# First pair's rows, key projections, query products and statistics computed in the setup's last stretch, whose steps get another order

## The reference

```python
def xattn(q, k, v, ...):                      # q = layernorm(x), k = v = ctx; layer_norm inside has gain and bias
    proj = lambda t: split_heads(layer_norm(t, ln_g, ln_b) @ w_in.T)       # 8 heads of 128
    f_q, f_k, f_v = proj(q), proj(k), proj(v)
    cosine_sim = einsum(f_q, f_k) / (|f_q| |f_k|)
    q_ratio, k_ratio = 2 * min(var, 1) / (var + 1) of f_q and f_k, per row and head
    var_component = q_ratio (x) k_ratio
    feat_corr = off-diagonal of (centered f_q)^T (centered f_q) / rows     # over ALL rows, per head
    decorr_scale = exp(-5 * norm(feat_corr) / D^2)
    h1 = relu(layer_norm([mean f_q, mean f_k] @ wp_w1.T + wp_b1)); weights = softmax(h1 @ wp_w2.T + wp_b2)
    mixed = w0 * cosine_sim + w1 * cosine_sim * decorr_scale + w2 * var_component
    return (mixed @ f_v) @ w_out.T + b_out
x = x + tanh(g_xattn) * xattn(layernorm(x), ctx, ctx)
x = x + tanh(g_ffn) * ffn(layernorm(x))       # 16-head softmax attention over pairs of batches (512 rows), two l2
                                              # normalisations and a gelu behind it
```

## Time and profile before

| | us |
|---|---|
| median of 3 runs (1323.11 to 1327.89) | 1324.99 |
| the profiled execution, its own time | 1325.61 |
| its span | 1323.9 |
| PE busy in the span | 1186.1 (90%) |
| DVE busy | 1066.7 (81%) |
| ACT busy | 1008.6 (76%) |
| POOL busy | 291.5 (22%) |

### The profile page before, as it was taken

The page is one execution under the profiler, slowest core; times in us unless marked ns, Lnnn a source line. Parts: engine busy times, 40 slices in busy tenths (PEclk is TensorE's granted clock), DMA queues, the critical chain, the costliest instruction groups (busy, mean ns, idle before and its releaser), DMA issues.

```text
span 1323.9 us, 34712 instructions
## 1 busy us (share of the span) xinstructions
PE 1186.1 (90%) x10322; PEld 748.6 (57%) x10322; DVE 1066.7 (81%) x3084; ACT 1008.6 (76%) x3333; POOL 291.5 (22%) x257
## 2 busy tenths in 40 slices
PE   4999967899999989898989898989898989898865
PEld 2677546564656565656565555656565656564521
DVE  5986635788888897988888888988888889898864
ACT  5768213296969696969797978888887889797887
POOL 1444103212212130303131212122222222222200
PEclk9999877999999999999999999999999999999987
DMA  8450014272727181818181827263635454454550
GB/s 259 135 168 22 4 37 96 89 168 83 186 67 202 48 221 42 213 46 216 45 212 37 207 59 203 66 190 79 181 88 170 99 159 110 148 121 147 108 160 17
DMA packets 247888, 162.30 MB, mean 123 GB/s; under 512 B 94538, under 2 KB 235559, under 8 KB 247848
## 3 DMA queue, kind: packets, MB, share of 16 engines
q1 hardware_dynamic: 247848, 161.80, 45.6%
HBM read 86.74 MB, written 42.58 MB: 98 GB/s over the span
## 4 chain that ended last, share of the span: by engine, by line
PE 66%; ACT 10%; issue 6%; DVE 3%; DMA 1%; ACTq 0%; SPq 0%; POOL 0%; POOLq 0%; PEldq 0%; DVEq 0%
PE work L894 18%; PE work L896 16%; PE work L895 16%; PE attended L1448 8%; PE score L1437 4%; ACT prob L1534 3%; PE work L1345 2%; ACT L1534 1%; ACT L1558 1%; ACT Gh L1507 1%; ACT zb L1558 1%; DVE wqTl L1634 1%; ACT wqTh L1493 1%; ACT VTh L1507 1%; ACT v L1520 1%
## 5 line engine op out<-in xcount | busy, mean ns | idle before, releaser
L1534 ACT ACTIVATE prob<-score,nm 128x256 f32<-128x256 f32 x1024 | 481.4, 495 | 18.6 <-DVE nm L1731 14.7
L1731 DVE TENSOR_REDUCE nm<-score 128x2 f32<-128x512 f32 x512 | 336.8, 680 | 9.3 <-PE score L1437 9.0
L1534 ACT ACTIVATION_READ_ACCUMULATOR prob<-score,nm 128x1 f32 x1024 | 232.7, 227 | 0.0
L1591 POOL TENSOR_TENSOR mTl<-md,mTh 128x512 f16<-128x512 f32 (+1 forms) x96 | 95.2, 998 | 357.9 <-ACT mTh L1507 357.9
L1448 PE MATMUL attended<-prob,vsp 128*32 128x256 f32 x2048 | 137.4, 392 | 1.9 <-DVE vsp L1746 1.0
L1649 DVE BATCH_NORM_STATS2 qst<-work 128x6 f32<-128x128 f32 x512 | 111.5, 281 | 12.0 <-PE work L896 11.9
L1437 PE MATMUL score<-qstack,kstack 64*128 64x256 f16 x1024 | 97.5, 279 | 18.7 <-ACT prob L1534 13.0
L1603 POOL TENSOR_TENSOR nrs<-nrm,phalf 128x8 f32<-128x8 f32 x16 | 26.3, 1642 | 352.7 <-ACT zb L1554 352.7
L894 PE MATMUL work<-wTh,xTh 128*128 128x512 f16 x256 | 98.1, 383 | 6.1 <-DVE xTl L1643 3.5
L895 PE MATMUL work<-wTl,xTh 128*128 128x512 f16 x256 | 97.8, 382 | 0.0
L896 PE MATMUL work<-wTh,xTl 128*128 128x512 f16 x256 | 97.8, 382 | 0.0
(11 more groups left out here) (327 smaller groups left out, 3216.4 us busy)
## 6 DMA issues: line engine op xcount, KB each, us to landing
qstack<-parts SPq DMA_DIRECT2D x64, 256.0 KB, 3.3
kstack<-parts SPq DMA_DIRECT2D x64, 256.0 KB, 3.8
sqE<-sq_rows SPq DMA_DIRECT2D x64, 154.0 KB
s_xin<-in_x SPq DMA_DIRECT2D x8, 1024.0 KB, 6.1
xin<-in_x SPq DMA_DIRECT2D x16, 512.0 KB, 3.6
x2S<-in_x SPq DMA_DIRECT2D x16, 512.0 KB, 3.6
parts<-qh SPq DMA_DIRECT2D x32, 256.0 KB, 2.5
parts<-ql SPq DMA_DIRECT2D x32, 256.0 KB, 2.7
```

Source lines behind the costliest of these rows:

```text
L1534: nc.scalar.activation(prob[:, g % PG, e, j + jj, :], sc[n % SC][:, jj * NQ:(jj + 1) * NQ], ACT.Exp, bias=nm[:, u + jj:u + jj + 1], accum_ ...
L1591: nc.gpsimd.tensor_tensor(dst, src, emptied(e[:2], "h")[0], ALU.subtract).then_inc(m_ready, 1)
L1731: nc.vector.tensor_reduce(nm[:, u:u + 2], sc[n % SC][:, :].rearrange("p (u q) -> p u q", q=NQ), AX.X, ALU.max, negate=True).then_inc(max_r ...
```

## The change

The first pair's `z`, `zT0`, `zT1`, `fk0` to `fk2` and `q0` to `q7` are taken out of `HEAD` and written out in the setup's last stretch, as `first_zT`, `first_fk`, `first_q` and `first_xT`, on PE, ACT and DVE. Their results (`norm`, `xTf`, `qst`, `fk`, `xT`) are kept from one phase to the other. The two query banks are `t_ps[1]` and `gram_ps[0]` in turn. What used `t_ps[1]` moves to parts of `t_ps[0]`.

The steps of the stretch get another order. On PE: turned rows, `wof`, spread, the three key projections, `keys0`, `lower`, `hm0`, `hm1`, `fe`, `keys1`, `h1`, `corr0`, `turned0`, q0, `corr1`, `turned1`, `h1T`, q1, `logits`, `kzT`, q2, `norms`, `last`, q3, `ku`, q4, `mix`, q5, `kr`, q6, q7. `key_sums` alternates between the two halves of 64 columns. On DVE all five `split_rest` come after `wof`, and the statistics of q0 to q7 stand between the links of the chain, those of q6 ahead of the last low half (`kr`) and those of q7 behind it. In the main phase the semaphores that those steps had raised are raised by SP at the start, and the turning of `rk` moves from behind `fk2` to behind `V3`.

```diff
+    w["norm"], w["xTf"], w["qst"] = kept("norm", [P, PT, DIM]), kept("xTf", [P, PR]), kept("qst", [P, PT, H, 6])
+    w["fk"] = {half: kept("fk" + half, [P, 2 * HM], F16) for half in "hl"}
+    w["xT"] = {half: kept("xT" + half, [P, KT, PR], F16) for half in "hl"}
...
+    FIRST_BANKS = {"zT0": t_ps[1][:, :], "zT1": f_ps[:, 0, :], "fk0": t_ps[1][:, :], "fk1": f_ps[:, 1, :],
+                   "fk2": f_ps[:, 2, :], **{f"q{c}": (t_ps[1], gram_ps[0])[c % 2][:, :] for c in range(2 * PT)}}
...
+            def first_q(c):
+                dve.wait_ge(first_filled, 6 + c)
+                for h in range(4):
+                    last = nc.vector.bn_stats(w["qst"][:, c // 2, 4 * (c % 2) + h, :],
+                                              first_bank(f"q{c}")[:, h * DH:(h + 1) * DH])
+                last.then_inc(first_low, 1)
...
+            dve.wait_ge(w["x_ready"], 16)
+            for t in range(PT):
+                last = nc.vector.tensor_scalar(w["norm"][:, t, :], w["xin"][:, t, :], w["stats"][:, t, 0:1],
+                                               w["stats"][:, t, 1:2], ALU.subtract, ALU.mult)
+            last.then_inc(rows_ready, 1)
             dve.wait_ge(pe_step, PE_TAIL["gram"])
...
+            for n in range(len(LATER)):
+                split_rest(n)
...
+            def first_xT(c, part):
+                act.wait_ge(first_filled, c + 1)
+                if part == "f":
+                    act.wait_ge(first_low, c)
+                nc.scalar.activation(w["xT"]["h"][:, c, :] if part == "h" else w["xTf"][:], first_bank(f"zT{c}"), ACT.Identity,
+                                     scale=w["gcol"][:, c:c + 1], bias=w["bcol"][:, c:c + 1]).then_inc(first_high, 1)
...
+            def first_q(c):
+                t, half = c // 2, c % 2
+                pe.wait_ge(first_low, 3 if c == 0 else 4 + c)
+                for k in range(KT):
+                    last = products(nc, first_bank(f"q{c}"), w["xT"], (ALL, k, slice(t * P, (t + 1) * P)),
+                                    w["wT"], (ALL, k, slice(half * 512, (half + 1) * 512)), k == 0, k == KT - 1)
+                last.then_inc(first_filled, 1)
+
+            pe.wait_ge(rows_ready, 1)
+            first_zT(0)
+            pe.wait_ge(f_used, NG * CG + START)
+            first_zT(1)
...
-            for h in range(H):
-                for k in range(KT):
-                    last = nc.tensor.matmul(t_ps[1][:, DIM + 2 * h:DIM + 2 * h + 2], full["wT"][:, k, h * DH:(h + 1) * DH],
-                                            sums[:, k, :], start=(k == 0), stop=(k == KT - 1))
-            reached("fe", last)
+            pe.wait_ge(first_high, 2)
+            first_fk(0)
+            first_fk(1)
+            first_fk(2)
 
             def key_sums(n):
 
-                for half in range(2):
-                    i = 2 * n + half
-                    for t in range(CG):
+                for t in range(CG):
+                    for half in range(2):
+                        i = 2 * n + half
...
             pe.wait_ge(wc_ready, 1)
+            pe.wait_ge(first_low, 5)
...
-            turn_keys(0)
-            pe.wait_ge(step, DVE_TAIL["h1"])
-            reached("h1T", nc.tensor.transpose(t_ps[0][:, 0:H], h1[:], w["ident"][0:H, 0:H]))
             pe.wait_ge(hm_ready, KT)
             pe.wait_ge(kr_act, 1)
             correlate(0)
-            pe.wait_ge(step, DVE_TAIL["h1T"])
-            reached("logits", nc.tensor.matmul(t_ps[1][0:H, 0:3], h1T[:], w2T_sb[:], start=True, stop=True))
+            turn_keys(0)
+            first_q(0)
             pe.wait_ge(kr_act, 2)
             correlate(1)
             turn_keys(1)
+            pe.wait_ge(step, DVE_TAIL["h1"])
+            reached("h1T", nc.tensor.transpose(t_ps[0][:, DH:DH + H], h1[:], w["ident"][0:H, 0:H]))
+            pe.wait_ge(step, DVE_TAIL["fcsum0"])
+            first_q(1)
+            pe.wait_ge(step, DVE_TAIL["h1T"])
+            reached("logits", nc.tensor.matmul(t_ps[0][0:H, DH + H:DH + H + 3], h1T[:], w2T_sb[:], start=True, stop=True))
...
             last.then_inc(kr_pe, 1)
+            first_q(6)
+            first_q(7)
...
 HEAD = """
-fk0 fk1 fk0.h fk1.h fk0.l fk1.l fk2 V1 ldx fk2.h z fk2.l V1.h V1.l zT0 zT0.h zT0.f zT0.l zT1 zT1.h zT1.f zT1.l q0 q0.o
-q1 q2 q1.o q2.o q3 q3.o q4 q4.o q5 q6 +ldx q5.o V0 q6.o q7 q7.o V0.h V3 qs1 G4 V0.l G4.h G0 G4.l G3 V3.h V3.l qpow
-G0.h G3.h G0.l G3.l +G1 qs2 +a0 +G5 +rk +a0.v +z +a0.h +G5.h +a0.l +G5.l +aux +V5 +G1.h +G2 +wq +G2.h +G2.l +G1.l +V2
...
+V1 ldx V1.h V1.l +ldx V0 V0.h V3 qs1 G4 V0.l G4.h G0 G4.l G3 V3.h V3.l qpow G0.h G3.h G0.l G3.l +G1 qs2 +a0 +G5 +rk
++a0.v +z +a0.h +G5.h +a0.l +G5.l +aux +V5 +G1.h +G2 +wq +G2.h +G2.l +G1.l +V2 +V2.h +sqe0 +sqe1 +fk0 +V2.l +d0 +fk0.h
...
+            sp.sem_inc(z_ready, 1)
+            sp.sem_inc(st_ready, 1)
+            sp.sem_inc(xT_ready, KT)
+            sp.sem_inc(hi_ready[lead("fk0.h")], 3)
...
-                if e == "fk2" and isinstance(a, int) and a == 0:
+                if e == "V3" and isinstance(a, int) and a == 0:
```

More of the change, by code:

```diff
@@ L576, in _ @@
             dve.wait_ge(pe_step, PE_TAIL["mix"])
-            link(nc.vector.tensor_copy(mix[:].rearrange("p a h -> p (a h)"), t_ps[0][:, 0:3 * H]))
+            link(nc.vector.tensor_copy(mix[:].rearrange("p a h -> p (a h)"), t_ps[0][:, 2 * DH - 3 * H:2 * DH]))
             dve.wait_ge(act_step, 4)
@@ L788, in _ @@
             key_sums(0)
-            pe.wait_ge(step, DVE_TAIL["fe"])
-            reached("lower", nc.tensor.transpose(t_ps[1][:, 0:P], gram[:, 0, P:DIM], w["ident"][:]))
-            for k in range(2):
-                last = nc.tensor.matmul(t_ps[0][0:H, DIM:DIM + DH], fe[:, k, :], w1T_sb[:, k, :], start=(k == 0), stop=(k == 1))
-            reached("h1", last)
+            pe.wait_ge(step, DVE_TAIL["gram"])
+            reached("lower", nc.tensor.transpose(t_ps[0][:, DIM:DIM + P], gram[:, 0, P:DIM], w["ident"][:]))
             pe.wait_ge(wc_ready, 1)
+            pe.wait_ge(first_low, 5)
             for m in range(KT):
@@ L806, in _ @@
                 reached(f"hm{m}", last)
+            for h in range(H):
+                for k in range(KT):
+                    last = nc.tensor.matmul(t_ps[0][:, DIM + P + 2 * h:DIM + P + 2 * h + 2], full["wT"][:, k, h * DH:(h + 1) * DH],
+                                            sums[:, k, :], start=(k == 0), stop=(k == KT - 1))
+            reached("fe", last)
             key_sums(1)
+            pe.wait_ge(step, DVE_TAIL["fe"])
+            for k in range(2):
+                last = nc.tensor.matmul(t_ps[0][0:H, 0:DH], fe[:, k, :], w1T_sb[:, k, :], start=(k == 0), stop=(k == 1))
+            reached("h1", last)
             def turn_stats(dst, i, t):
@@ L849, in _ @@
             reached("kzT", last)
-            pe.wait_ge(step, DVE_TAIL["fcsum1"])
-            reached("norms", nc.tensor.matmul(t_ps[0][:, DIM:DIM + H], ones[:], fcs[:], start=True, stop=True))
+            first_q(2)
+            pe.wait_ge(step, DVE_TAIL["ladd"])
+            reached("norms", nc.tensor.matmul(t_ps[0][:, DH + 2 * H:DH + 3 * H], ones[:], fcs[:], start=True, stop=True))
             for i in range(NG):
@@ L1191, in pass_over @@
                     t, s = waiting[slot].pop(0)
-                    assert not 0 <= t - lead(s) < NPAIR
+                    assert not 0 <= t - lead(s) < NPAIR or (t == lead(s) and s in FIRST)
                     left_out.append((t, s))
@@ L1195, in pass_over @@
                     passed(left_out)
+            present = {(first + (token[0] == "+"), plain(token)) for token in order}
+            for slot in range(WORK):
+                pass_over(slot, next(use for use in waiting[slot] if use in present))
             for token in order:
```

147 lines of the change are left out of this document (95 added, 52 removed).

## The result

| | before | after |
|---|---|---|
| median of the runs (lowest to highest), us | 1325.18 (1322.91 to 1327.89), 6 runs | 1313.74 (1311.36 to 1315.56), 6 runs |
| profiled execution, its span, us | 1325.61, 1323.9 | 1315.56, 1313.8 |
| ratio, 95% interval | | 0.9913 [0.9899, 0.9927] |

The kernel is 11.4 us faster by the medians; the forecast was 1314.6 and its own range 1312 to 1318. The profiled execution of after is its slowest run, so its trace shows a little less of the gain, 10.05 us.

The account below looks back on a forecast made before the run. PE was taken to bound the loop and the setup's last stretch, a dependency chain the main phase's start. Gate gain -20.7 plus setup growth 10.3 gave -10.4 us: 1314.6 us, own range 1312 to 1318.

Parts of the forecast that it names:

- The gate: Main phase's start: POOL's power waits for the second transposing transfer, 12.2 us in instead of 32.9; gain 20.7 us.
- PE idle from 12 to 18 us, at no cost: Main phase's start: PE has nothing then, but the stretch behind `aux` stays the same as before.
- Rows, keys, queries: Setup's last stretch: moved work adds 1.1, 3.3 and 10.4 us on PE, together 14.8; two filled waits return 2.5.
- The key sums: Setup: alternating halves overlap, 2.2 us each instead of 3.75 and 5.38; gain 3.1 us for both (0 to 5.1).
- The clock behind `ku`: Setup: PE's clock falls inside `ku`, slowing q4 and q5; cost 1.0 us (0 to 5.2).
- Given back: Setup: PE waits of 1.34 and 1.19 us filled, 2.5; q6 and q7 behind `kr` at the end, 0.4 us back.
- PE's one wait before `logits`: Setup: PE waits for DVE once, since `h1T` is copied behind the second correlation; cost 0.5 us.
- SP's own end "some 3 us before DVE does": Setup's end: SP's transfers of `rk` and the fixed row, behind `ku` on ACT, end some 3 us before DVE.
- The shift goes through to the end: Main phase behind `aux`: same as before, step for step, so the earlier power's whole gain reaches the kernel's end.
- rivals, 1 and 2: Slower setup: handovers with low clock, 16 to 19 us growth (0.13); half clock through all queries, 25 to 26 (0.05).
- Rival 1: Setup: query handovers and low clock through q4 to q7, growth 16 to 19 us, 1319 to 1323; chance 0.13.
- Rival 3: Gate opens earlier or the start is tighter: another 3 to 5 us, 1310 to 1312; chance 0.09.

Follow-up runs that it names:

- e1: Changed kernel with POOL's wait for the two transposing transfers moved from its first step to behind the first power; 1308.68 us, ratio to before 0.9883.
- e3: Changed kernel with the key sums in the old order, one half of 64 columns after the other; 1315.23 us, ratio 0.9932.
- e2: As e1, and the load of the second pair's rows issued ahead of SP's wait for the stored kr rows; 1304.29 us, ratio 0.9852.
- e7: Changed kernel without the first pair's work in the setup, its buffers filled with ones; new order and alternating key sums kept; 1304.12 us, ratio 0.986.
- e9: As e4, with ACT's copy of the last turned row ahead of its copy of `ku`; 1304.67 us, ratio 0.9849.
- e5: Changed kernel with the eight head means put one or two at a time between the products of `hm`; 1310.92 us, ratio 0.9897.
- e4: Changed kernel without the first pair's eight query products and their statistics, `qst` filled with ones; 1308.49 us, ratio 0.9878.
- e8: e2 and e5 in one, with the product `h1` ahead of the second key sum; 1302.18 us, ratio 0.9842.
- e10: As e8, with ACT's copy of the last turned row ahead of its copy of `ku`; 1303.9 us, ratio 0.9837.

## Why the prediction was right

Forecast -10.4 us, measured -10.05 in the two profiled executions and -11.4 by the medians. The mechanism is the one told: a later start of the main phase for a much earlier power. That the number is within 0.4 us is partly luck: 0.8 too much in the setup stands against 0.8 too little at the gate, and 1.7 us won ahead of the change and 0.5 behind `aux` against 2.5 us lost behind the first `md`, most of them in the loop's first turn. By its steps:

- **The gate.** Predicted 12.2 us into the phase (11.5 to 12.9), a gain of 20.7; measured 11.4 and 21.5, released by the transfer named. The term was 0.8 too small, and the power is 0.1 ahead of my lower bound. Landing counts from the issue's start (2.74 us), the earlier of the two ends that I gave. The first transpose is issued 7.27 us behind the phase's first product (184.57 - 177.30), where before it was 7.31; counted to SP's first transfer it was 6.52 and is 7.04, so the queue is 0.5 us slower, which the later first product hides. By that count the gain is 20.9. e1 showed that the gate was real.
- **PE idle from 12 to 18 us, at no cost.** PE is idle at 190 to 192, and `aux` to `md` didn't get longer (12.21 against 12.75).
- **Rows, keys, queries.** 14.8 us predicted. The keys took 3.3 (128.25 to 131.54), the rows 0.9 (I had 1.1). For the queries 10.4 less 2.5 of filled waits gives 7.9; the runs showed 7.7.
- **The key sums.** Predicted -3.1 at full clock; -2.7 by e3 (2.39 us a sum, where I had 2.2). But this is the term that failed in size: I said that the clock's fall behind the means would move onto the second sum "and costs about the same". Before, the means and both sums took 3.63 + 5.38 + 3.75 = 12.8 us. In after's profile they take 4.56 + 4.55 + 2.39 = 11.5, because the clock fell earlier, inside the means. So the three gave back 1.3 and not 3.1. Where it doesn't fall (e2) they take 8.4 and give back 4.4. In e7 and e9, where it fell a little later, they take 10.1 and 10.0 and give back 2.7. My number lies inside this range, and the execution decides.
- **The clock behind `ku`.** Predicted 1.0. q4, `mix` and q5 take 4.73 us in after (166.52 to 171.25); e5, at full clock, had the next step, `kr`, 3.3 us ahead of after's (167.99 against 171.25, with the Gram matrix 1.6 us later and 3.1 us saved at the means), so about 1.8 us are lost to it.
- **Given back.** These two make the growth 2.6 us larger than the sum. 0.9 of it came back in `kr`, which takes 0.77 us in one piece (171.25 to 172.02) and had waited for its inputs before (161.93 to 164.79, of which I had counted 1.2 as given back). Of the rest, about 1 us, 0.6 is the later first product of the new phase: counted to SP's first transfer the stretch grew by 10.6, against a forecast of 10.3. The last 0.4 I can't place.
- **PE's one wait before `logits`.** Predicted 0.5, measured 0.90 on `h1T`.
- **SP's own end "some 3 us before DVE does".** True in after: the store's issue ends at 170.08, DVE at 175.87. But I had not seen it as a floor. It hid 2.2 us of what e4 took away, and my expectation of e4 failed on it (and on my 9 to 11 us for queries that cost 7.7). The working took DVE's `krl` as the end of the old stretch, and there too the store was later (167.0 against 166.23).
- **The shift goes through to the end.** Not quite in this execution: of the 12.6 us at `md`, 13.2 at the loop's first load, 11.0 were left behind the first turn, in which the clock was at half for some 3 us, and 10.05 at the end. Five kernels with the same main phase have no such fall. That the fall is the whole of the loss is argued, not shown.

Of the rivals, 1 and 2 (handovers, the clock at half through all queries) did not come: q0 to q3 ran at full clock, 1.3 us each. (Rival 1's growth of 16 to 19 us is 1320 to 1323 by its own sum, not 1319.) Rival 3, in which the change itself is 3 to 5 us faster, did not come either; e1 and e2 show that this much and more lay behind the gate, but it took further edits.

## What to carry to other kernels

When a chain is moved out of a phase, look next at what else stands in front of its end, and put each wait at the instruction that needs it: one wait moved and one transfer issued earlier (e2) brought the first `md` 7.3 us nearer to the phase's start, where the whole change had brought 11.4 us of time. A kernel's stretches can end on a small store whose issue waits behind an unrelated copy; it can stay unseen until the work above it is gone, so when you price a step by leaving it out, look at what the stretch then ends on. A run of 32 narrow matmuls cost more than its own time here, in most executions. And a profile is one execution: the same code's stretch differed by 3.3 us between two of them, which is more than most of the single terms of this forecast.

## What the hardware did that I had not expected

- PE's clock fell from 2.4 to 1.2 GHz while PE was busy without a gap, inside 32 matmuls of two columns. With this order and the means in one run it fell there or right behind in five profiles (after, e1, e4, e7, e9) and not in two (e2, e3); before, it fell behind them too; with the means spread it didn't in three of three (e5, e8, e10). By the 5 in 7 alone three in a row without a fall would come about once in 40 times, so the spreading is likely but not surely the cause. A fall costs 1.6 to 3.3 us (the means and the second key sum together take 7.65 to 9.3 us instead of 6.0).
- Twenty f32 passes of 257 columns with 64-column weights take 3.75 us one half after the other and 2.39 us alternating between the two halves, at the same clock.
- From DVE's end to the next phase's first product it was 1.4 to 1.6 us where DVE ended the stretch, and 3.8 us where a small store did (e4, e7); of these, 2.4 us are SP's wait for the store behind its issue.
